# Two mixture-of-experts stages: a tile's biases copied on chip by a compute engine instead of fetched by two transfers

## The chip, the cores and the metric

The kernel runs on one core of one Trainium2 chip. The time is the device time of that core in microseconds (us), from repeated runs; 2293.36 us is the median before (3 runs, 2291.95 to 2298.7). A core has TensorE (PE in the profile: matrix products; PEld is its loading of weights), VectorE (DVE), ScalarE (ACT), GpSimd (POOL) and SyncE (SP), each with its own instruction queue in order, and 16 DMA engines that move what the queues issue. Engines wait for each other by counting semaphores.

## What is computed

A network of two blocks on an image batch of 8 x 128 channels x 32 x 32, 8192 tokens of 128 numbers. Each block has a convolutional attention part and a mixture of 8 experts, in which each token goes to its two best experts. Cut to the experts:

```
# block 0, for each token and its two experts e, weighted by its gate
h = x @ w1[e] + b1[e]
y = (silu(h @ wg[e] + bg[e]) * (h @ wv[e] + bv[e])) @ w2[e] + b2[e]
# block 1
y = gelu(x @ w1[e] + b1[e]) @ w2[e] + b2[e]
```

## The kernel before

The kernel is a chain of stages with a barrier behind each: project, attend and route (block 0), **experts** (layer 0), combine and convolve, attend and route (block 1), **experts** (layer 1), combine and store. `experts` (L1104) is one function that runs twice; `second` tells the layers apart. Below, the first experts stage is layer 0 and the second is layer 1.

The routing stage has written every token, once for each of its two experts, as a row of 130 numbers into `xd_dram`, sorted by expert into tiles of `SLOT` = 256 rows. There are `TILES` = 71 tiles. A table in on-chip memory gives for tile j the expert (row 0) and the place of its rows (row 1). The weights of all 8 experts lie on chip in `wres`, and so do their biases: `biases` (128 x 8 x 4) for the first product and `down_biases` (128 x 8 x 128) for the second. In layer 0 w1 is multiplied into wg and wv beforehand, so both layers have an up-projection from 128 to 4 x 128 and a down-projection back (from 2 x 128 in layer 0, from 4 x 128 in layer 1).

For each tile j, with ring place r = j mod 8 and parity p = j mod 2:

- **SP** (`load`, L1158): reads the expert e and the place u from the table into registers (L1159, L1160), then issues three transfers into ring place r: `rec[:, r, 0:4]` from `biases` (L1161), `rec[:, r, 4:]` from `down_biases` (L1162), `xr[:, r]` from `xd_dram` (L1163). All three count on the semaphore `loaded[r]`, 16 each, so `LOADS` = 48 (L1124). The first 8 loads go out at once; the load for tile j + 8 waits until `yo` of tile j is ready (L1170).
- **TensorE** transposes the tile (`turn`, L1181, waits for `loaded[r]`), multiplies by the four up blocks (`first`, L1191, waits for `xt_copied` and `w_copied`), and by the down blocks (`finish`, L1205, after a register load of e at L1206).
- **The up copy** (`turn` of ScalarE in layer 0, L1225; of VectorE in layer 1, L1250): the tile's up block of weights, 128 x 512, from `wres` to `up[:, p]`, after a register load of e (L1222, L1247). It raises `w_copied`. In layer 1 it stands in VectorE's queue ahead of the `xt` copy.
- **VectorE** copies the transposed tile to `xt` (L1256, in layer 1 with the norm's scale and shift, L1253).
- **ScalarE** applies silu (L1238) or gelu (L1233) with the bias from `rec`; in layer 0 VectorE adds the second bias from `rec` and multiplies (L1265).
- **VectorE** (`finish`, L1269) adds the down bias from `rec[:, r, 4:]` (L1271), takes the rows' places (L1274) and multiplies by the gates into `yo` (L1276); **GpSimd** sends `yo` to its places by two indirect transfers (L1286).

What sets the order is `over_tiles` (L1126): every engine but SP and GpSimd runs, tile by tile, `first` of tile j + 1, `turn` of tile j + 2, `finish` of tile j. So a tile is transposed and its up block copied two steps before it is finished:

```
            for r in range(RING):
                at(first, group, r + 1)
                at(turn, group, r + 2)
                at(finish, group, r)
```

Of the kernel before, what the change touches and what calls it, by code (L numbers as in the profile page):

```python
# [9 lines left out]
ACT = mybir.ActivationFunctionType  # L10
# [294 lines left out]
E = 8  # L305
# [47 lines left out]
def attend_and_route_first(nc, sb, sem, bank, w, X, XF, stacks0, parts_dram, v_dram, xd_dram, table, resident, to_fold, down):  # L353
# [66 lines left out]
    def wide(t):  # L420
        return t[:].unsqueeze(2).to_broadcast([C, G, E])
    LOADS = 16 * (len(Q_PARTS) + len(K_PARTS))

# [21 lines left out]
    with nc.Block() as block:  # L445
# [90 lines left out]
        def _(pe):  # L536
# [4 lines left out]
            def take_max(b, par, k, slot):  # L541

                h, c, half = k // 16, k // 2 % TC, k % 2
                if k % 64 == 0:
                    pe.wait_ge(qk_loaded[k // 64], b * LOADS)
                pe.matmul(bank[:, slot, :], qs[par][0:KB, h, c * C:(c + 1) * C],  # L546
# [557 lines left out]
def experts(nc, sb, sem, bank, w, layer, xd_dram, yd_dram, table, resident):  # L1104

    second = layer == 1
    wres, biases, down_biases = resident
    NH = 4 if second else 2
    W2 = 4 * C
    rec = sb("rec", [C, RING, BIASES], F32)  # L1110
    up = sb("up", [C, 2, 4 * C], F32)
# [7 lines left out]
    loaded = [sem(f"loaded{r}") for r in range(RING)]  # L1119
    turned, xt_copied, g_ready, v_ready, gated = sem("turned"), sem("xt_copied"), sem("g_ready"), sem("v_ready"), sem("gated")  # L1120
    w_copied = sem("w_copied")
    h_ready, y_ready, y_copied, yo_ready, held = sem("h_ready"), sem("y_ready"), sem("y_copied"), sem("yo_ready"), sem("held")
    sent = [sem("sent0"), sem("sent1")]
    LOADS = 16 * 3  # L1124

    def over_tiles(eng, turn, first, finish):  # L1126

        def at(step, group, r):
            group, r = group + r // RING, r % RING
            step(RING * group + r, r, r % 2, RING // 2 * group + r // 2, group)

        last = (TILES - 1) // RING
        at(turn, 0, 0)
        at(first, 0, 0)
        at(turn, 0, 1)
        with eng.Fori(0, last) as group:
# [4 lines that stand above are left out]
        left = TILES - last * RING  # L1144
        for r in range(left):
            if r + 1 < left:
                at(first, last, r + 1)
            if r + 2 < left:
                at(turn, last, r + 2)
            at(finish, last, r)  # L1150

    def nothing(*_):
        pass

    with nc.Block() as block:
        @block.sync
        def _(sp):
            def load(j, r):  # L1158
                e = sp.value_load(table[0:1, 0, bass.ds(j, 1)], min_val=0, max_val=E - 1)  # L1159
                u = sp.value_load(table[0:1, 1, bass.ds(j, 1)], min_val=0, max_val=UNITS_XD - 1)  # L1160
                sp.dma_start(rec[:, r, 0:4], biases[:, bass.ds(e, 1), :].rearrange("c o n -> c (o n)")).then_inc(loaded[r], 16)  # L1161
                sp.dma_start(rec[:, r, 4:], down_biases[:, bass.ds(e, 1), :].rearrange("c o n -> c (o n)")).then_inc(loaded[r], 16)  # L1162
                sp.dma_start(xr[:, r].rearrange("t q r -> t (q r)"),  # L1163
                             xd_dram[bass.ds(u * SLOT, SLOT), :].rearrange("(t q) r -> t (q r)", q=SQ)).then_inc(loaded[r], 16)

            for r in range(RING):
                load(r, r)

            def load_next(i, r):
                sp.wait_ge(yo_ready, RING * i + r + 1)  # L1170
                load(RING * (i + 1) + r, r)

            with sp.Fori(0, TILES // RING - 1) as i:
                for r in range(RING):
                    load_next(i, r)
            for r in range(TILES % RING):
                load_next(TILES // RING - 1, r)

        @block.tensor
        def _(pe):  # L1180
            def turn(j, r, p, h, i):  # L1181
                pe.wait_ge(loaded[r], (i + 1) * LOADS)
                pe.wait_ge(xt_copied, 2 * h)
                for q in range(SQ):
                    ins = pe.transpose(bank[:, p, q * C:(q + 1) * C], xr[:, r, q, 0:C], w["ident"])
                ins.then_inc(turned, 1)
# [30 lines left out]
        @block.scalar  # L1217
        def _(act):
            def turn(j, r, p, h, i):
                if second:  # L1220
                    return
                e = act.value_load(table[0:1, 0, bass.ds(j, 1)], min_val=0, max_val=E - 1)  # L1222
                if not (isinstance(j, int) and j < 2):
                    act.wait_ge(h_ready, (j - 1) * NH)
                act.activation(up[:, p], wres[:, bass.ds(e, 1), 0:W2].rearrange("c o n -> c (o n)"), ACT.Copy).then_inc(w_copied, 1)  # L1225

            def first(j, r, p, h, i):
                if not (isinstance(j, int) and j == 0):
                    act.wait_ge(y_ready, j - 1)
                for f in range(NH):  # L1230
                    act.wait_ge(g_ready, j * NH + f + 1)
                    if second:
                        act.activation(hidden[:, p, f, :], bank[:, 2 + f, 0:SLOT], ACT.Gelu,  # L1233
                                       bias=rec[:, r, f:f + 1]).then_inc(h_ready, 1)
                    else:
                        if f == 0:
                            act.wait_ge(h_ready, j * 2)
                        act.activation(gate[:, f, :], bank[:, 2 + 2 * f, 0:SLOT], ACT.Silu,  # L1238
                                       bias=rec[:, r, 2 * f:2 * f + 1]).then_inc(gated, 1)

            over_tiles(act, turn, first, nothing)

        @block.vector
        def _(dve):
            def turn(j, r, p, h, i):
                if second:
                    e = dve.value_load(table[0:1, 0, bass.ds(j, 1)], min_val=0, max_val=E - 1)  # L1247
                    if not (isinstance(j, int) and j < 2):
                        dve.wait_ge(h_ready, (j - 1) * NH)
                    dve.tensor_copy(up[:, p], wres[:, bass.ds(e, 1), 0:W2].rearrange("c o n -> c (o n)")).then_inc(w_copied, 1)  # L1250
                dve.wait_ge(turned, j + 1)
                if second:
                    dve.tensor_scalar(xt[:, p, :], bank[:, p, 0:SLOT], w["ln"][:, 0:1], w["ln"][:, 1:2],  # L1253
                                      ALU.mult, ALU.add).then_inc(xt_copied, 1)
                else:
                    dve.tensor_copy(xt[:, p, :], bank[:, p, 0:SLOT]).then_inc(xt_copied, 1)  # L1256

            def first(j, r, p, h, i):
                if not second:
                    if not (isinstance(j, int) and j == 0):  # L1260
                        dve.wait_ge(y_ready, j - 1)
                    for f in range(2):
                        dve.wait_ge(gated, j * 2 + f + 1)
                        dve.wait_ge(v_ready, j * 2 + f + 1)
                        dve.scalar_tensor_tensor(out=hidden[:, p, f, :], in0=bank[:, 3 + 2 * f, 0:SLOT],  # L1265
                                                 scalar=rec[:, r, 2 * f + 1:2 * f + 2], in1=gate[:, f, :],
                                                 op0=ALU.add, op1=ALU.mult).then_inc(h_ready, 1)

            def finish(j, r, p, h, i):  # L1269
                dve.wait_ge(y_ready, j + 1)  # L1270
                dve.tensor_tensor(y1[:, p], bank[:, 6 + p, 0:SLOT].rearrange("t (q c) -> t q c", q=SQ),  # L1271
                                  rec[:, r, 4:].unsqueeze(1).to_broadcast([C, SQ, C]), ALU.add).then_inc(y_copied, 1)
                dve.wait_ge(sent[p], h * (16 * SQ))
                dve.tensor_scalar(places[:, p], xr[:, r, :, C + 1], 0.0, None, ALU.add)  # L1274
                dve.wait_ge(y_copied, j + 1)
                dve.tensor_tensor(yo[:, p], y1[:, p], xr[:, r, :, C:C + 1].to_broadcast([C, SQ, C]), ALU.mult).then_inc(yo_ready, 1)  # L1276

            over_tiles(dve, turn, first, finish)
# [1012 lines left out]
def metaformer(nc, x_in, columns, weights, to_fold, rest0, rec1, toeplitz, out):  # L2291
# [31 lines left out]
    with ExitStack() as ctx:  # L2323
# [6 lines left out]
        with ExitStack() as own:  # L2330
            mine = allocator(own, nc.sbuf_tensor)
            XF, biases = mine("XF", [C, TOKENS], F32), mine("biases", [C, E, 4], F32)
            resident = (XF[:, 0:6 * T].rearrange("c (e k) -> c e k", e=E), biases[:],
                        XF[:, 6 * T:7 * T].rearrange("c (e k) -> c e k", e=E))
            with ExitStack() as first:
                stacks0 = [allocator(first, nc.sbuf_tensor)(name, [KM, HEADS, T], BF16)[:] for name in ("qs0", "ks0")]
                stage(normalize_and_project, X, XF, stacks0, parts_dram, v_dram)
                stage(attend_and_route_first, X, XF, stacks0, parts_dram, v_dram, xd_dram[0], table, resident, to_fold, rest0)
            stage(experts, 0, xd_dram[0], yd_dram[0], table, resident)
# [121 lines left out]
```

## Time and profile before

| | |
|---|---|
| runs, median (lowest to highest) | 2293.36 us (2291.95 to 2298.7) |
| the profiled execution: span | 2495.0 us, 41046 instructions |
| mean granted clock of TensorE | 0.887 of full speed |
| TensorE, VectorE, ScalarE, GpSimd busy | 80%, 57%, 44%, 30% of the span |
| the experts stages, layer 0 and layer 1 | about 1235 to 1520 us and 2131 to 2445 us of the span |

The profile shows one execution, recorded with all its instructions; for this one no other time than its span is shown, and it is longer than the runs that were timed without recording. Times in a timeline count from the span's start. A timeline row gives start, length, engine (SPq is the queue of SyncE), line of the kernel, operation, what is written and read, and in brackets the engine's idle time before it with what ended it. Register loads, waits and other instructions of the queues alone don't show in it. TensorE's products are pipelined and the ends of their rows are modelled; a run of them on one line is one row, with its count. A row of a group gives the line, the shapes, how many, the busy time in us, the mean length of one in ns, and the idle time ahead of them.

### The profile page before, as it was taken

How to read it: one execution, taken by the hardware profiler on the slowest of the kernel's cores; microseconds unless marked ns; L12 is line 12 of the kernel's file. 1: busy time of each engine (PE TensorE's matmuls, PEld its weight loads, DVE VectorE, ACT ScalarE, POOL GpSimd, SP SyncE). 2: the span in 40 equal slices, each digit the busy share in tenths (PEclk: the TensorE clock that was granted, in tenths of full speed). 3: DMA queues.
4: the chain of work that ended last, by engine and by line, in shares of the span. 5: the costliest groups of instructions: out<-in, count | busy, mean ns of one | idle time of the engine just before them, and what ended most of it. 6: DMA issues, size and time to landing. Idle time of an engine off the chain costs nothing. (4 is left out here: it accounts for less than half of the span.)

```text
span 2495.0 us, 41046 instructions
## 1 busy us (share of the span) xinstructions
PE 2001.3 (80%) x13306; PEld 1090.0 (44%) x13307; DVE 1432.7 (57%) x3154; ACT 1092.3 (44%) x1682; POOL 753.8 (30%) x883
## 2 busy tenths in 40 slices
PE   5759999898999899986588886986597871699894
PEld 2421223232232223223376664654365541588883
DVE  4779888686878687713155555742444453234444
ACT  4530666564656465763133443431143431334343
POOL 1240003332333334243244552000004445345442
PEclk9865999998999899987699998999889885799996
DMA  3844132323232322011333333222011321232325
GB/s 133 201 169 68 19 51 26 60 27 60 27 60 26 60 32 55 16 40 58 93 83 83 88 89 119 76 93 67 8 36 50 107 60 56 69 80 76 82 68 213
DMA packets 134782, 180.00 MB, mean 72 GB/s; under 512 B 44592, under 2 KB 87856, under 8 KB 132336
## 3 DMA queue, kind: packets, MB, share of 16 engines
q1 hardware_dynamic: 116208, 138.25, 23.3%
q0 software_dynamic: 18432, 39.88, 4.7%
q8 instruction: 87, 1.43, 0.2%
q14 instruction: 55, 0.45, 0.1%
HBM read 99.04 MB, written 69.01 MB: 67 GB/s over the span
## 5 line engine op out<-in xcount | busy, mean ns | idle before, releaser
L775 DVE TENSOR_REDUCE mx<-bank 128x1 f32<-128x512 f32 x1024 | 640.3, 696 | 140.3 <-PE bank L546 90.3
L722 ACT ACTIVATE P<-bank 128x1024 f32<-128x1024 f32 x512 | 498.0, 1021 | 412.9 <-PE bank L648 327.0
L546 PE MATMUL bank<-ks,qs 96*128 96x512 bf16 x1024 | 374.6, 415 | 62.7 <-DVE mx L775 44.3
L1286 POOL DMA_INDIRECT results<-yo,places x284 | 273.9, 964 | 359.6 <-DVE yo L1276 274.8
L648 PE MATMUL bank<-qs,ks 99*128 99x512 bf16 x1024 | 310.9, 387 | 14.3 <-ACT P L722 13.2
L1202 PE MATMUL bank<-xt,up 128*128 128x256 f32 x1136 | 286.6, 397 | 41.9 <-DVE xt L1253 20.8
L628 PE MATMUL bank<-P,vt 128*32 128x512 f32 x2048 | 277.5, 614 | 1.6 <-ACT P L722 1.6
L2285 POOL DMA_INDIRECT dispatched<-planes,places x128 | 123.1, 962 | 479.0 <-DVE stats L2129 356.3
L1202 PEld LDWEIGHTS bank<-xt,up 128*128 128x128 f32 x1136 | 211.6, 196 | 76.8 <-issue 36.0
L546 PEld LDWEIGHTS bank<-ks,qs 96*128 96x128 bf16 x1024 | 100.8, 99 | 305.7 <-DVE mx L775 204.0
L648 PEld LDWEIGHTS bank<-qs,ks 99*128 99x128 bf16 x1024 | 77.4, 98 | 299.1 <-ACT P L722 195.9
L1233 ACT ACTIVATE hidden<-bank,rec 128x256 f32<-128x256 f32 x284 | 121.0, 474 | 185.6 <-PE bank L1202 164.9
L995 POOL TENSOR_TENSOR a<-o,den 128x512 f32<-128x512 f32 x32 | 40.5, 1264 | 346.0 <-ACT den L710 322.8
L1211 PE MATMUL bank<-planes,hidden 128*128 x1136 | 141.8, 279 | 0.9 <-DVE y L1271 0.7
L1271 DVE TENSOR_TENSOR y<-bank,rec 128x256 f32<-128x256 f32 x142 | 60.1, 423 | 143.1 <-PE bank L1211 86.4
L1045 POOL DMA_INDIRECT dispatched<-outgoing,places x128 | 123.8, 967 | 44.9 <-issue 41.7
L1211 PEld LDWEIGHTS bank<-planes,hidden 128*128 128x128 f32 x1136 | 136.1, 196 | 1.4 <-issue 1.3
L1238 ACT ACTIVATE gate<-bank,rec 128x256 f32<-128x256 f32 x142 | 66.1, 473 | 149.5 <-PE bank L1202 102.2
L1713 PE MATMUL bank<-planes,bands 32*32 32x248 f32 (+2 forms) x3840 | 85.6, 394 | 43.0 <-issue 27.6
L1265 DVE SCALAR_TENSOR_TENSOR hidden<-bank,rec,gate 128x256 f32<-128x256 f32 x142 | 67.6, 483 | 61.9 <-ACT gate L1238 22.1
L1734 DVE STREAM_TRANSPOSE planes<-out 128x1024 f32<-128x1024 f32 x24 | 43.7, 1895 | 99.5 <-ACT out L1726 99.5
L1211 PE MATMUL bank<-XF,hidden 128*128 x568 | 80.5, 285 | 21.6 <-DVE hidden L1265 12.1
(298 smaller groups left out, 2582.3 us busy)
## 6 DMA issues: line engine op xcount, KB each, us to landing
xr<-dispatched SPq DMA_DIRECT2D x142, 130.0 KB
qk_parts<-parts SPq DMA_DIRECT2D x16, 768.0 KB, 5.1
qs<-qk_parts SPq DMA_DIRECT2D x84, 128.0 KB
ks<-qk_parts SPq DMA_DIRECT2D x84, 128.0 KB
v_turned<-vt SPq DMA_DIRECT2D x8, 1024.0 KB, 5.6
vt<-v_turned SPq DMA_DIRECT2D x8, 1024.0 KB
bands<-results SPq DMA_DIRECT2D x32, 256.0 KB, 3.8
y<-results SPq DMA_DIRECT2D x32, 256.0 KB
```

The costliest lines, as they stand in the source:

```text
L546: pe.matmul(bank[:, slot, :], qs[par][0:KB, h, c * C:(c + 1) * C], ks[par][0:KB, h, half * HALF:(half + 1) * HALF], start=True, stop=True) ...
L628: ins = pe.matmul(bank[32 * j:32 * j + 32, 4, :], vt[:, par, s, head * VH:(head + 1) * VH], P[:, (2 * e + j // 2) % SLOTS, j % 2 * HALF:(j ...
L648: ins = pe.matmul(bank[:, 2 * pair + u, :], ks[par][:, head, s * C:(s + 1) * C], qs[par][:, head, n * HALF:(n + 1) * HALF], start=True, st ...
L722: act.activation(P[:, x % SLOTS, :], bank[:, 2 * pair:2 * pair + 2, :] .rearrange("p a t -> p (a t)"), ACT.Exp).then_inc(probs_ready, 1)
L775: dve.tensor_reduce(mx[:, k // 2, k % 2:k % 2 + 1], bank[:, slot, :], AX.X, ALU.max).then_inc(unit_freed, 1)
L1045: pool.indirect_dma_start(xd_dram, bass.IndirectOffsetOnAxis(places[:, q, k:k + 1], 0), outgoing[:, q, k, :], None).then_inc(sent, 16)
L1202: ins = pe.matmul(bank[:, 2 + f, 0:SLOT], up[:, p, f * C:(f + 1) * C], xt[:, p, :], start=True, stop=True)
L1211: ins = pe.matmul(bank[:, 6 + p, q * C:(q + 1) * C], hidden[:, p, f, q * C:(q + 1) * C], weights(e, W2 + f * C), start=(f == 0), stop=(f = ...
L1233: act.activation(hidden[:, p, f, :], bank[:, 2 + f, 0:SLOT], ACT.Gelu, bias=rec[:, r, f:f + 1]).then_inc(h_ready, 1)
L1286: pool.indirect_dma_start(yd_dram, bass.IndirectOffsetOnAxis(places[:, p, q:q + 1], 0), yo[:, p, q, :], None).then_inc(sent[p], 16)
L1713: ins = pe.matmul(sums[:, :, y0:y1], bands[rows, m * TAPS + dy, :], plane[:, :, y0 + dy - PAD:y1 + dy - PAD], start=(dy == DY_ORDER[0]), s ...
L2285: pool.indirect_dma_start(xd_dram, bass.IndirectOffsetOnAxis(places[:, p, q, k:k + 1], 0), rows[p][:, q, k, :], None).then_inc(sent[p], 16)
```

## The change

The two transfers of `rec` and SP's register load of e are gone, and `LOADS` is 16. A new function `take_biases` copies the same two pieces, 128 x 4 and 128 x 128, from the resident biases to `rec[:, r]`. The engine that makes the up copy calls it right behind that copy, ScalarE in layer 0 (as an activation with the function Copy) and VectorE in layer 1 (as a tensor copy). `w_copied` is now raised by the second of the two copies instead of the up copy.

```
--- before.py
+++ after.py
@@ -1121,7 +1121,7 @@
     w_copied = sem("w_copied")
     h_ready, y_ready, y_copied, yo_ready, held = sem("h_ready"), sem("y_ready"), sem("y_copied"), sem("yo_ready"), sem("held")
     sent = [sem("sent0"), sem("sent1")]
-    LOADS = 16 * 3
+    LOADS = 16
 
     def over_tiles(eng, turn, first, finish):
 
@@ -1149,6 +1149,11 @@
                 at(turn, last, r + 2)
             at(finish, last, r)
 
+    def take_biases(copy, e, r):
+
+        copy(rec[:, r, 0:4], biases[:, bass.ds(e, 1), :].rearrange("c o n -> c (o n)"))
+        return copy(rec[:, r, 4:], down_biases[:, bass.ds(e, 1), :].rearrange("c o n -> c (o n)"))
+
     def nothing(*_):
         pass
 
@@ -1156,10 +1161,7 @@
         @block.sync
         def _(sp):
             def load(j, r):
-                e = sp.value_load(table[0:1, 0, bass.ds(j, 1)], min_val=0, max_val=E - 1)
                 u = sp.value_load(table[0:1, 1, bass.ds(j, 1)], min_val=0, max_val=UNITS_XD - 1)
-                sp.dma_start(rec[:, r, 0:4], biases[:, bass.ds(e, 1), :].rearrange("c o n -> c (o n)")).then_inc(loaded[r], 16)
-                sp.dma_start(rec[:, r, 4:], down_biases[:, bass.ds(e, 1), :].rearrange("c o n -> c (o n)")).then_inc(loaded[r], 16)
                 sp.dma_start(xr[:, r].rearrange("t q r -> t (q r)"),
                              xd_dram[bass.ds(u * SLOT, SLOT), :].rearrange("(t q) r -> t (q r)", q=SQ)).then_inc(loaded[r], 16)
 
@@ -1222,7 +1224,8 @@
                 e = act.value_load(table[0:1, 0, bass.ds(j, 1)], min_val=0, max_val=E - 1)
                 if not (isinstance(j, int) and j < 2):
                     act.wait_ge(h_ready, (j - 1) * NH)
-                act.activation(up[:, p], wres[:, bass.ds(e, 1), 0:W2].rearrange("c o n -> c (o n)"), ACT.Copy).then_inc(w_copied, 1)
+                act.activation(up[:, p], wres[:, bass.ds(e, 1), 0:W2].rearrange("c o n -> c (o n)"), ACT.Copy)
+                take_biases(lambda to, of: act.activation(to, of, ACT.Copy), e, r).then_inc(w_copied, 1)
 
             def first(j, r, p, h, i):
                 if not (isinstance(j, int) and j == 0):
@@ -1247,7 +1250,8 @@
                     e = dve.value_load(table[0:1, 0, bass.ds(j, 1)], min_val=0, max_val=E - 1)
                     if not (isinstance(j, int) and j < 2):
                         dve.wait_ge(h_ready, (j - 1) * NH)
-                    dve.tensor_copy(up[:, p], wres[:, bass.ds(e, 1), 0:W2].rearrange("c o n -> c (o n)")).then_inc(w_copied, 1)
+                    dve.tensor_copy(up[:, p], wres[:, bass.ds(e, 1), 0:W2].rearrange("c o n -> c (o n)"))
+                    take_biases(dve.tensor_copy, e, r).then_inc(w_copied, 1)
                 dve.wait_ge(turned, j + 1)
                 if second:
                     dve.tensor_scalar(xt[:, p, :], bank[:, p, 0:SLOT], w["ln"][:, 0:1], w["ln"][:, 1:2],
```

## Rows read from the trace of the kernel before

**Rows 1.** Windows by stage: busy us (and instructions) of each engine, PE clock, DMA share, GB/s.

```profile
1235.00:1520.00 285.00, 231.64 (x1278) 191.07 (x1278) 153.84 (x426) 112.03 (x214) 134.96 (x141) 0.96 0.31 83
...
2131.00:2445.00 314.00, 283.05 (x1846) 257.34 (x1846) 129.29 (x355) 122.28 (x285) 136.51 (x141) 0.95 0.28 75
```

**Rows 2.** Timeline of ScalarE, first stage: start, length, line, tiles [idle before, its releaser].

```profile
1251.55 0.47 ACT L1238 ACTIVATE gate<-bank,rec 128x256 f32<-128x256 f32 x1 [0.39 <-PE bank L1202]
1252.28 0.63 ACT L1225 ACTIVATE up<-XF 128x512 f32 x1 [0.26 <-issue]
```

**Rows 3.** Timeline of TensorE over the same tile.

```profile
1249.95 1.99 PE L1202 MATMUL bank<-xt,up 128*128 128x256 f32 x8
...
1253.15 1.56 PE L1202 MATMUL bank<-xt,up 128*128 128x256 f32 x6
```

**Rows 4.** Timeline of VectorE over the same tile.

```profile
1252.46 0.41 DVE L1256 COPY xt<-bank 128x256 f32<-128x256 f32 x1
```

**Rows 5.** Timeline of TensorE: first and last of the short distances.

```profile
1246.76 1.99 PE L1202 MATMUL bank<-xt,up 128*128 128x256 f32 x8 [0.70 <-DVE xt L1256]
...
1508.95 1.99 PE L1202 MATMUL bank<-xt,up 128*128 128x256 f32 x8
```

**Rows 6.** Timeline of SP's queue, start of the first stage.

```profile
1236.93 0.60 SPq L1161 DMA_DIRECT2D rec<-biases  x1
...
1238.42 0.43 SPq L1163 DMA_DIRECT2D xr<-dispatched  x1
1240.12 0.51 SPq L1161 DMA_DIRECT2D rec<-biases  x1
...
1243.18 0.50 SPq L1161 DMA_DIRECT2D rec<-biases  x1
```

**Rows 7.** Timeline of TensorE, start of the first stage.

```profile
1240.69 0.69 PE L1185 MATMUL bank<-weights,xr 128*128 128x128 f32 x2 [6.53 <-DMA xr<-dispatched]
```

**Rows 8.** Timeline of SP's queue, late in the first stage.

```profile
1417.94 0.50 SPq L1161 DMA_DIRECT2D rec<-biases  x1
...
1434.41 0.45 SPq L1163 DMA_DIRECT2D xr<-dispatched  x1
1436.61 0.50 SPq L1161 DMA_DIRECT2D rec<-biases  x1
```

**Rows 9.** Timeline of TensorE, late in the first stage.

```profile
1436.79 0.44 PE L1185 MATMUL bank<-weights,xr 128*128 128x128 f32 x2
```

**Rows 10.** Groups of ScalarE by shape: busy us, mean ns of one, idle before.

```profile
L1225 ACT ACTIVATE up<-XF 128x512 f32 x71 | 44.7, 630 | 19.7 <-issue 14.7 <-PEq L2315 3.5 <-DVE hidden L1265 1.4
...
L174 ACT ACTIVATE bqk<-weights 128x2 f32<-128x2 f32 x1 | 0.2, 203 | 7.5 <-PEq L2315 7.5
```

**Rows 11.** Groups of VectorE by shape.

```profile
L2113 DVE COPY ln_bias<-weights 128x128 f32<-128x128 f32 x1 | 0.2, 219 | 0.0
...
L2111 DVE COPY base<-weights 128x8 f32<-128x8 f32 x1 | 0.2, 159 | 0.0
```

**Rows 12.** Timeline of TensorE, second stage, two places.

```profile
2332.51 1.89 PE L1202 MATMUL bank<-xt,up 128*128 128x256 f32 x8
...
2336.25 1.89 PE L1202 MATMUL bank<-xt,up 128*128 128x256 f32 x8
...
2432.11 1.92 PE L1202 MATMUL bank<-xt,up 128*128 128x256 f32 x8
```

**Rows 13.** Timeline of VectorE, second stage, the same places.

```profile
2334.38 0.43 DVE L1250 COPY up<-planes 128x512 f32 x1 [0.42 <-ACT hidden L1233]
2334.72 0.54 DVE L1253 TENSOR_SCALAR xt<-bank,weights 128x256 f32<-128x256 f32 x1
...
2431.44 0.54 DVE L1253 TENSOR_SCALAR xt<-bank,weights 128x256 f32<-128x256 f32 x1
```

**Rows 14.** Timeline of ScalarE, second stage, a disturbed stretch.

```profile
2346.30 0.47 ACT L1233 ACTIVATE hidden<-bank,rec 128x256 f32<-128x256 f32 x1 [1.07 <-PE bank L1202]
2347.81 0.47 ACT L1233 ACTIVATE hidden<-bank,rec 128x256 f32<-128x256 f32 x1 [1.04 <-DMA bands<-toeplitz]
```

More of the change, by code:

```diff
@@ L1123, in experts @@
     sent = [sem("sent0"), sem("sent1")]
-    LOADS = 16 * 3
+    LOADS = 16
     def over_tiles(eng, turn, first, finish):
@@ L1150, in over_tiles, with take_biases @@
             at(finish, last, r)
+    def take_biases(copy, e, r):
+        copy(rec[:, r, 0:4], biases[:, bass.ds(e, 1), :].rearrange("c o n -> c (o n)"))
+        return copy(rec[:, r, 4:], down_biases[:, bass.ds(e, 1), :].rearrange("c o n -> c (o n)"))
     def nothing(*_):
@@ L1158, in load @@
             def load(j, r):
-                e = sp.value_load(table[0:1, 0, bass.ds(j, 1)], min_val=0, max_val=E - 1)
                 u = sp.value_load(table[0:1, 1, bass.ds(j, 1)], min_val=0, max_val=UNITS_XD - 1)
-                sp.dma_start(rec[:, r, 0:4], biases[:, bass.ds(e, 1), :].rearrange("c o n -> c (o n)")).then_inc(loaded[r], 16)
-                sp.dma_start(rec[:, r, 4:], down_biases[:, bass.ds(e, 1), :].rearrange("c o n -> c (o n)")).then_inc(loaded[r], 16)
                 sp.dma_start(xr[:, r].rearrange("t q r -> t (q r)"),
@@ L1224, in turn @@
                     act.wait_ge(h_ready, (j - 1) * NH)
-                act.activation(up[:, p], wres[:, bass.ds(e, 1), 0:W2].rearrange("c o n -> c (o n)"), ACT.Copy).then_inc(w_copied, 1)
+                act.activation(up[:, p], wres[:, bass.ds(e, 1), 0:W2].rearrange("c o n -> c (o n)"), ACT.Copy)
+                take_biases(lambda to, of: act.activation(to, of, ACT.Copy), e, r).then_inc(w_copied, 1)
             def first(j, r, p, h, i):
@@ L1249, in turn @@
                         dve.wait_ge(h_ready, (j - 1) * NH)
-                    dve.tensor_copy(up[:, p], wres[:, bass.ds(e, 1), 0:W2].rearrange("c o n -> c (o n)")).then_inc(w_copied, 1)
+                    dve.tensor_copy(up[:, p], wres[:, bass.ds(e, 1), 0:W2].rearrange("c o n -> c (o n)"))
+                    take_biases(dve.tensor_copy, e, r).then_inc(w_copied, 1)
                 dve.wait_ge(turned, j + 1)
```

## The prediction

> **What bounds the kernel now.** The windows by stage come first: the first experts stage lasts 285.00 us and the second 314.00 us of the span of 2495.0 us, at granted clocks of 0.96 and 0.95, so the upper of the two levels (2.4 GHz) nearly throughout [rows 1]. In the second, TensorE is busy for 283.05 of 314.00 us; in the first for 231.64 of 285.00 [rows 1]. Nothing outside these two stages is touched, so both are read tile by tile.
>
> In an undisturbed tile of the first stage, the chain runs over ScalarE. The up-projection starts at 1249.95 [rows 3]; the second gate starts at 1251.55 and ends at 1252.02, 2.07 us later; after 0.26 us for the register that holds the expert's number, the up copy runs from 1252.28 to 1252.91 [rows 2]; the next up-projection starts at 1253.15, 0.24 us behind it [rows 3]. That is 3.20 us per tile, all of it ScalarE's turn. VectorE's `xt` copy, the other operand, ends at 1252.87 [rows 4], only 0.04 us earlier.
>
> Later in the same stage something else shows. The queue of SP (SyncE) issues three transfers per tile. At the start it takes 3.06 us per tile with nothing to wait for (from 1240.12 to 1243.18) [rows 6]; later five tiles take from 1417.94 to 1436.61, 3.73 us each [rows 8]. There it has lost its lead: the 52nd `xr` is issued at 1434.41 [rows 8], and the 52nd pair of transposes starts at 1436.79, 2.4 us behind [rows 9], about the time that the first issue needs (1238.42 to 1240.69) [rows 6, 7]. So in this execution SP sets the pace over much of the stage.
>
> Is this pace that of the timed runs? The timed median is 2293.36 us; the profiled execution's span is 201.6 us longer. A stretch of the second stage shows where such time sits: ScalarE, with its operands long issued, starts activations of 0.47 us at 2346.30 and 2347.81, 1.51 us apart [rows 14]. I take these stalls, SP's extra 0.67 us per tile (3.73 less 3.06) among them, to belong to the recording, and the undisturbed tiles to the timed runs. The Trainium skill (Runtime: NRT & Kernel Launch, section The ~15µs preamble/postamble breakdown) states a gap of about 6.2 us that doesn't depend on the kernel; this trace disagrees with 201.6 us, but by that rule SP's pace would be real, which is the first rival below.
>
> **The change, part by part.** *Removed:* per tile, two issues and one register load on SP, and 66 KB of moving inside the on-chip memory. SP keeps one register load and one issue. From the start of the first issue to that of the third is 1.49 us (1236.93 to 1238.42); the two register loads lie in the 1.27 us between the third issue's end at 1238.85 and 1240.12, so one is 0.64 [rows 6]. The first `xr` of a stage is thus issued 2.1 us earlier, and the first transposes, which wait for nothing else (6.53 us, ended by that transfer [rows 7]), move with it. The second stage begins with the same pattern, once. What would be late next, the table load and the first up copy on the engine beside, ends before the first projection needs it. I take 1.95 us per stage: **-3.9 us**; bounds 0 and -4.2. Where SP isn't the pace, its remaining relief is worth nothing: it hides behind a tile of 3.20 us against SP's 3.06. The removed bytes are worth nothing either: the DMA engines are busy for 0.31 and 0.28 of the stages [rows 1].
>
> *Added in the first stage, on ScalarE:* two copies, 128x4 and 128x128, behind the up copy, with `w_copied` moved behind the second. The trace has no such copies of these sizes. The nearest are a 128x2 copy at 203 ns and the 128x512 one at 630 [rows 10]; a straight line between them gives about 205 and 310 ns, 0.51 us one after the other. But queued instructions overlap: on VectorE a copy of 0.43 us is followed 0.34 us later by the next [rows 13]. With some 0.1 us of overlap at each of two joints it is 0.28 to 0.31; I take **0.28 us**, since nothing separates the three copies but address arithmetic that the queue does while the 0.63 us copy runs. Behind them on ScalarE waits the next tile's gate, which waits for TensorE anyway; TensorE's own queue, in order, holds at `w_copied` the next up-projection, the transposes and the register load of the down-projection. So the chain goes from 3.20 to 3.48 us.
>
> How often does this count? At most for all 71 tiles: 71 x 0.28 = 19.9 us. At least where the profiled execution already has tiles closer than 3.47 us: 26 of the 70 distances between up-projections (the first begins at 1246.76, the last at 1508.95 [rows 5]), which fall short of it by 6.6 us together. I take the middle, **+13.3 us**: the timed runs should hold fewer disturbed tiles than the profile, but not none.
>
> *Added in the second stage, on VectorE:* the same two copies behind its up copy and ahead of `xt`. A 128x8 copy takes 159 ns and a 128x128 one 219 [rows 11]; less 0.09 at each joint that is 0.20 us, at worst 0.38. TensorE is the pace here: tiles start 3.74 us apart (2332.51 to 2336.25), while `xt`, begun at 2334.72, ends at 2335.26, 0.99 us ahead of its use [rows 12, 13]. That cover hides 0.20 us. Where VectorE runs late it is gone: another `xt` ends at 2431.98 and its projection starts at 2432.11 [rows 12, 13]. If every second tile were so, it would cost 35 x 0.20 = 7 us. I take **0**, as in the undisturbed tiles.
>
> Sum: -3.9 + 13.3 + 0 = +9.4 us. Against the profiled execution that is 2495.0 to 2504.4, and since the costs are in undisturbed tiles I add them whole to the median of the runs: 2293.36 + 9.4 = **2302.8 us**.
>
> **The rivals.** *SP's pace is real: faster.* If the timed runs also take 3.73 us per tile over some 50 tiles of the first stage [rows 8], the change replaces that by ScalarE's 3.48: 50 x 0.25 = 12.5 us less, and 3.9 at the starts: 2277 us. For it speaks the 2.4 us lead in rows 8 and 9; against it the 3.06 us that SP needs undisturbed [rows 6]. It decides from 3.48 us per tile on SP. Chance 0.22.
>
> *The copies are hidden: no change.* If only the 26 short distances count, the sum is +6.6 - 3.9 = +2.7: 2296 us. For it speaks that the stage's mean, 285.00/71 = 4.0 us [rows 1], has 0.5 us of room above 3.48; against it that a serial chain gives room only to those tiles that something else held up. Chance 0.28.
>
> *The copies don't overlap: clearly slower.* At 0.51 us on every tile it is 71 x 0.51 = 36.2, less 3.9: +32, 2326 us. The Trainium skill (VectorE: DVE Perf Modes, section The TRN2 errata — SBUF-src ops pay a fixed extra latency per instruction) speaks for it, and against this change: an instruction that reads SBUF pays a fixed cost exposed between instructions, so many small ones pay it each; its figures give an estimate of 0.48 us for the two copies on ScalarE, +30 us in all. The overlap in rows 13 disagrees. Chance 0.10.
>
> **How the numbers follow.** My own case, slower by 7 to 16 us, has 0.40. About 0.3%, 6.9 us, is what a measurement here can tell from no change. Faster by more: 0.22. Within: 0.28 of the hidden case. Slower: 0.40 + 0.10 = 0.50. The range reaches from the middle of the first rival, 2277 us, to short of the last, 2322 us (half of VectorE's worst on top of 19.9 and some lost overlap); about 0.1 lies out on each side. The likeliest case alone is 2298 to 2312 us.
>
> **What would show it.** Right: SP's two issues per tile gone, the first transposes of either stage 2 us earlier after SP's first register load; two new ScalarE groups of 71, near 0.2 and 0.3 us; the last copy of a tile ending some 0.9 us after its up copy began; and the shortest repeated distance of up-projections in the first stage 3.48 us where it is 3.20 now, with no transposes that wait for `xr`. In the second stage distances of 3.74 us as before. Wrong: if that shortest distance stays near 3.2 us, the copies cost nothing; if it is 3.7, they don't overlap; if the timed runs are faster although it is 3.48, SP was the pace in them.

## The result and the profile after

| | before | after |
|---|---|---|
| runs, median (lowest to highest) | 2292.6 us (2286.59 to 2299.22, 20 runs) | 2297.47 us (2293.47 to 2305.41, 20 runs) |
| ratio to before, 95% interval | | 1.0025 (1.0016 to 1.0033) |
| profiled execution: span | 2495.0 us | 2296.0 us (its own time 2297.84) |

The change makes the kernel 4.9 us slower by the medians. That is inside the 0.3% that the prediction called "within", on the side it forecast, and just below its likeliest case of 2298 to 2312 us.

The profile before was recorded on an execution some 200 us longer than the timed ones; this one agrees with the timed runs. Set side by side, the two spans would show a gain of 199 us that no timed run has. So "before" is read below from a second profile of the unchanged kernel (span 2283.4 us). First the changed kernel, in the windows of its two experts stages (columns as in [rows 1]):

```profile
1159.00:1420.00 261.00, 225.20 (x1297) 192.46 (x1296) 155.38 (x427) 134.75 (x357) 134.65 (x141) 0.99 0.25 73
...
1968.00:2250.00 282.00, 267.89 (x1846) 248.55 (x1846) 142.09 (x497) 126.61 (x285) 139.15 (x143) 0.98 0.23 67
```

One tile of the first stage, from the timeline of all engines (it answers [rows 2, 3]):

```profile
1284.27 1.99 PE L1204 MATMUL bank<-xt,up 128*128 128x256 f32 x8 [0.38 <-ACT rec L1228]
...
1285.86 0.47 ACT L1241 ACTIVATE gate<-bank,rec 128x256 f32<-128x256 f32 x1 [0.39 <-PE bank L1204]
...
1286.59 0.63 ACT L1227 ACTIVATE up<-XF 128x512 f32 x1 [0.25 <-issue]
1286.77 0.41 DVE L1260 COPY xt<-bank 128x256 f32<-128x256 f32 x1
1287.12 0.19 ACT L1228 ACTIVATE rec<-biases 128x4 f32 x1
1287.22 0.29 ACT L1228 ACTIVATE rec<-XF 128x128 f32 x1
1287.74 1.99 PE L1204 MATMUL bank<-xt,up 128*128 128x256 f32 x8 [0.38 <-ACT rec L1228]
```

The chain is the one of [rows 2, 3] with the two copies in it. The up copy begins at 1286.59, the last copy ends at 1287.51, 0.92 us later (forecast: some 0.9), and the next projection begins 0.23 us behind that. The distance is 3.47 us, and the bracket names the releaser: `rec`, at the line of the copies. Of the 70 distances of the stage 55 lie between 3.47 and 3.51 us. The groups of the new copies answer [rows 10, 11] (busy us, mean ns, idle before), first stage on ScalarE, second on VectorE:

```profile
L1228 ACT ACTIVATE rec<-XF 128x128 f32 x71 | 20.8, 293 | 0.0
L1228 ACT ACTIVATE rec<-biases 128x4 f32 x71 | 13.4, 189 | 0.0
```

```profile
L1155 DVE COPY rec<-planes 128x128 f32 x71 | 17.4, 245 | 0.1
L1154 DVE COPY rec<-planes 128x4 f32 x71 | 12.6, 177 | 0.0
```

The second stage (it answers [rows 12, 13]) keeps its pace. Its projections start 3.74 us apart, and `xt` ends at 2103.51, 0.65 us ahead of its use, though four instructions now stand where two were:

```profile
2100.42 1.89 PE L1204 MATMUL bank<-xt,up 128*128 128x256 f32 x8
2102.43 0.43 DVE L1253 COPY up<-planes 128x512 f32 x1 [0.92 <-ACT hidden L1236]
2102.77 0.16 DVE L1154 COPY rec<-planes 128x4 f32 x1
2102.84 0.44 DVE L1155 COPY rec<-planes 128x128 f32 x1
2102.97 0.54 DVE L1257 TENSOR_SCALAR xt<-bank,weights 128x256 f32<-128x256 f32 x1
2104.16 1.89 PE L1204 MATMUL bank<-xt,up 128*128 128x256 f32 x8
```

### The profile page after: what moved, and what is told of

Same layout as the page of the kernel before. It is cut to its first block and busy times, and to the rows that moved or that the text cites. A ratio compares the mean times of both kernels' runs of the same rounds, so it can differ in the third digit from the quotient of the medians.

```text
span 2296.0 us, 40508 instructions
## 1 busy us (share of the span) xinstructions
PE 1952.7 (85%) x13306; PEld 1076.5 (47%) x13307; DVE 1446.1 (63%) x3296; ACT 1119.5 (49%) x1824; POOL 756.3 (33%) x883
## 5 line engine op out<-in xcount | busy, mean ns | idle before, releaser
L1204 PE MATMUL bank<-xt,up 128*128 128x256 f32 x1136 | 278.7, 389 | 29.0 <-ACT rec L1228 26.1
L1204 PEld LDWEIGHTS bank<-xt,up 128*128 128x128 f32 x1136 | 207.0, 192 | 65.5 <-issue 38.0
L1717 PE MATMUL bank<-planes,bands 32*32 32x240 f32 (+2 forms) x3840 | 85.4, 392 | 42.2 <-issue 26.5
L1187 PE MATMUL bank<-weights,xr 128*128 128x128 f32 x284 | 54.9, 275 | 43.0 <-DMA xr<-dispatched 43.0
```

The source lines that it names most:

```text
L1204: ins = pe.matmul(bank[:, 2 + f, 0:SLOT], up[:, p, f * C:(f + 1) * C], xt[:, p, :], start=True, stop=True)
L1717: ins = pe.matmul(sums[:, :, y0:y1], bands[rows, m * TAPS + dy, :], plane[:, :, y0 + dy - PAD:y1 + dy - PAD], start=(dy == DY_ORDER[0]), s ...
```

## The experiments

**What did the kernel before do?** The unchanged kernel, profiled again; it took 2285.19 us in that run.

> The kernel before, unchanged, for a second profile. Theory A (the two queues take turns): in the changed kernel every tile of the first stage takes ScalarE's 3.48 us; the runs are 4.9 us apart in their medians, 3.9 of it given back at the starts, so the kernel before must average 3.48 less (4.9 + 3.9) / 70 = 3.35 us there, above ScalarE's 3.20 because SP's queue of three issues is the pace in the loop: distances all near 3.3, transposes that wait for xr, second stage 3.73. Theory B (disturbed tiles): distances of 3.20 in most tiles with single long ones between, which reach a mean near 3.35 by something that is not SP's queue. Theory C (SP as in the first profile): 3.73 in most tiles of the first stage, and the time is saved elsewhere.

First the start of the first stage in it, which answers [rows 6, 7], and then the same in the changed kernel:

```profile
1160.65 0.60 SPq L1161 DMA_DIRECT2D rec<-biases  x1
...
1162.14 0.43 SPq L1163 DMA_DIRECT2D xr<-dispatched  x1
1164.34 0.69 PE L1185 MATMUL bank<-weights,xr 128*128 128x128 f32 x2 [6.46 <-DMA xr<-dispatched]
1165.55 3.78 PE L1202 MATMUL bank<-xt,up 128*128 128x256 f32 x8 [0.52 <-DVE xt L1256]
```

```profile
1164.22 8.18 SPq L1165 DMA_DIRECT2D xr<-dispatched  x8
1166.35 0.69 PE L1187 MATMUL bank<-weights,xr 128*128 128x128 f32 x2 [4.40 <-DMA xr<-dispatched]
1167.55 3.45 PE L1204 MATMUL bank<-xt,up 128*128 128x256 f32 x8 [0.52 <-DVE xt L1260]
```

TensorE's wait falls from 6.46 to 4.40 us: 2.06 us gained (1.95 forecast). Then the queue of SP in the middle of the stage of the unchanged kernel, and TensorE beside it:

```profile
1288.93 0.43 SPq L1163 DMA_DIRECT2D xr<-dispatched  x1
...
1292.21 0.45 SPq L1163 DMA_DIRECT2D xr<-dispatched  x1
...
1295.99 0.43 SPq L1163 DMA_DIRECT2D xr<-dispatched  x1
...
1315.94 0.43 SPq L1163 DMA_DIRECT2D xr<-dispatched  x1
```

```profile
1289.88 1.91 PE L1202 MATMUL bank<-xt,up 128*128 128x256 f32 x8
1291.63 0.38 PE L1185 MATMUL bank<-weights,xr 128*128 128x128 f32 x2
1292.49 1.15 PE L1211 MATMUL bank<-XF,hidden 128*128 x8 [0.48 <-issue]
1293.48 1.89 PE L1202 MATMUL bank<-xt,up 128*128 128x256 f32 x8
...
1400.56 1.99 PE L1202 MATMUL bank<-xt,up 128*128 128x256 f32 x8
```

Eight loads, one turn of SP's loop, take from 1288.93 to 1315.94, 3.38 us each: 3.28 (1288.93 to 1292.21), and 3.78 across the loop's end (1292.21 to 1295.99). At the start, with nothing to wait for, a load takes 3.05 (3.06 in [rows 6]); in the loop each has a wait and its index arithmetic besides. The stage's up-projections run from 1165.55 to 1400.56, 235.01/70 = 3.36 us each. That is the 3.35 of theory A, and C falls: SP is the pace, at 3.38 us, not at the 3.73 of [rows 8]. The picture of B, most tiles at 3.20 us and single long ones, is not there either: in the loop short distances (3.1 to 3.3 us) and long ones (3.3 to 3.9 us) take turns.

Two signs of A failed with that: the distances are not all near 3.3 us, and the transposes show no wait for `xr`. The time stands elsewhere, as 0.48 us of "issue" ahead of the down products. The `xr` issued at 1288.93 has landed by the time TensorE itself is free for the transposes. But its queue was held by the wait for it until 1291.30, and the register load for the down products, next in that queue, begins at 1291.52; in the tile of the changed kernel shown above it begins at 1284.73, while the up-projection runs. (A queue's own instructions are in the trace, though the timeline leaves them out.) It is so in 48 tiles on end, the 17th to the 64th up-projection: the register load begins 2.27 to 2.63 us behind the issue of the `xr` that the queue waits for. In the changed kernel it begins some 16.5 us behind that issue, and 0.37 to 0.47 us behind the start of the up-projection. In the groups of TensorE in the first stage this idle time is there before, and gone after, where ScalarE's copies take its place:

```profile
L1211 PE MATMUL bank<-XF,hidden 128*128 x552 | 78.1, 284 | 13.8 <-issue 7.8 <-DVE hidden L1265 4.2
```

```profile
L1204 PE MATMUL bank<-xt,up 128*128 128x256 f32 x568 | 142.6, 395 | 27.6 <-ACT rec L1228 26.1 <-issue 1.1 <-DVE xt L1260 0.5
L1213 PE MATMUL bank<-XF,hidden 128*128 x552 | 72.9, 275 | 0.0
```

**The two halves of the change apart.** Three kernels made of the changed one. *Copies off the chain:*

```
-                act.activation(up[:, p], wres[:, bass.ds(e, 1), 0:W2].rearrange("c o n -> c (o n)"), ACT.Copy)
-                take_biases(lambda to, of: act.activation(to, of, ACT.Copy), e, r).then_inc(w_copied, 1)
+                act.activation(up[:, p], wres[:, bass.ds(e, 1), 0:W2].rearrange("c o n -> c (o n)"), ACT.Copy).then_inc(w_copied, 1)
+                take_biases(lambda to, of: act.activation(to, of, ACT.Copy), e, r).then_inc(b_copied, 1)
...
             def first(j, r, p, h, i):
                 if not (isinstance(j, int) and j == 0):
                     act.wait_ge(y_ready, j - 1)
+                if not second:
+                    act.wait_ge(b_copied, j + 1)
```

> The changed kernel with the two copies of the first stage off the chain: the up copy raises w_copied itself, the copies raise a semaphore of their own that ScalarE's gate waits for. Theory A: 3.20 us per tile where the changed kernel has 3.48, so 71 x 0.28 = 19.9 us less than its 2297.5: 2277.6 us, ratio to before 0.9935. Theory B: only the undisturbed tiles gain, at most half: about 2288, ratio 0.998. If the copies' time on ScalarE itself counts (the next gate is late), no gain: 2297, 1.002.

*Transfers kept,* into a tile that nothing reads, with `LOADS` at 48 again, so that TensorE waits for all three:

```
+    spare = sb("spare", [C, RING, BIASES], F32)
...
+                e = sp.value_load(table[0:1, 0, bass.ds(j, 1)], min_val=0, max_val=E - 1)
+                sp.dma_start(spare[:, r, 0:4], biases[:, bass.ds(e, 1), :].rearrange("c o n -> c (o n)")).then_inc(loaded[r], 16)
+                sp.dma_start(spare[:, r, 4:], down_biases[:, bass.ds(e, 1), :].rearrange("c o n -> c (o n)")).then_inc(loaded[r], 16)
```

> The changed kernel with SP's load of e and its two transfers kept, into a tile that nothing reads, so the copies are paid and nothing is removed. Theory A: 3.48 us per tile as in the changed kernel (SP's 3.3 is hidden behind it), and 1.95 us more at each start: 2297.5 + 3.9 = 2301.4, ratio to before 1.004. Theory C (SP takes 3.73 us per tile): 71 x 0.25 = 17.8 us more on top: 2319, ratio 1.011.

*Both edits:*

> Both edits: the transfers kept and the copies off the chain. Theory A: SP's pace as in the kernel before, about 3.35 us per tile, and its starts: 2292.6 us, ratio 1.000 (0.999 to 1.001). Theory B: the same time as the kernel with the copies off the chain plus 3.9 us.

Each cell has the median, the ratio to the runs of the kernel before that were taken beside it, with its interval, and the mean distance of up-projections in the first stage of the profile (last start less first, over 70):

| | copies ahead of `w_copied` | copies off the chain |
|---|---|---|
| transfers gone | the change: 2297.47 us, 1.0025 (1.0016 to 1.0033), 3.50 us | 2277.57 us, 0.9943 (0.9924 to 0.9962), 3.22 us |
| transfers kept | 2299.86 us, 1.0043 (1.0029 to 1.0056), 3.50 us | 2294.1 us, 1.0021 (1.0001 to 1.0040), 3.36 us |

Theory A holds in all four cells. With the copies on the chain SP's load is hidden: keeping it costs only the starts. SP's queue then runs ahead of TensorE at a pace of its own, which is 3.38 us again (eight loads in 27.00 us), and its lead over the transposes grows from 5.40 us at the 17th tile to 11.28 at the 65th:

```profile
1270.15 0.44 SPq L1169 DMA_DIRECT2D xr<-dispatched  x1
...
1297.15 0.43 SPq L1169 DMA_DIRECT2D xr<-dispatched  x1
```

With the copies off the chain, SP's load is the pace again, at 3.36 us as in the kernel before. Only with neither does the tile come to 3.22. The last kernel (transfers kept, copies off the chain) was expected at 1.000; its interval just leaves that out. One of its twelve runs, at 2316.99 us, is 21 us above all others and lifts the ratio; its first stage is that of the kernel before, and where the rest lies stays open. The tile with the copies off the chain and the transfers gone (the window ends within its last row):

```profile
1272.42 1.99 PE L1204 MATMUL bank<-xt,up 128*128 128x256 f32 x8
...
1274.74 0.63 ACT L1227 ACTIVATE up<-XF 128x512 f32 x1 [0.25 <-issue]
1274.92 0.41 DVE L1262 COPY xt<-bank 128x256 f32<-128x256 f32 x1
1275.27 0.19 ACT L1228 ACTIVATE rec<-biases 128x4 f32 x1
1275.37 0.29 ACT L1228 ACTIVATE rec<-XF 128x128 f32 x1
...
1275.60 1.77 PE L1204 MATMUL bank<-xt,up 128*128 128x256 f32 x7
```

The projection at 1275.60 starts 0.23 us behind the up copy's end (1275.37) and ahead of the last copy's end: 3.18 us, against 3.47 with the copies waited for. The copies' price is thus 0.29 us a tile.

**The number of issues, or the bytes?** Copies off the chain, as above, but only the 128x4 piece copied; the 128x128 piece (64 KB) stays SP's transfer, with its register load.

```
+                e = sp.value_load(table[0:1, 0, bass.ds(j, 1)], min_val=0, max_val=E - 1)
+                sp.dma_start(rec[:, r, 4:], down_biases[:, bass.ds(e, 1), :].rearrange("c o n -> c (o n)")).then_inc(loaded[r], 16)
...
     def take_biases(copy, e, r):
-        copy(rec[:, r, 0:4], biases[:, bass.ds(e, 1), :].rearrange("c o n -> c (o n)"))
-        return copy(rec[:, r, 4:], down_biases[:, bass.ds(e, 1), :].rearrange("c o n -> c (o n)"))
+        return copy(rec[:, r, 0:4], biases[:, bass.ds(e, 1), :].rearrange("c o n -> c (o n)"))
```

> Copies off the chain as in the earlier run, but only the 128x4 piece is copied; the large piece (64 KB) stays a transfer of SP, with SP's load of e. If the pace of the kernel before is the number of issues on SP's queue (3.38 us per tile in the loop of the second profile, one issue 0.65), SP needs 2.73 us per tile, less than ScalarE's 3.20, and the whole gain of the loop stays: 2277.6 us and 1.35 us more at each start, 2280.3, ratio to before 0.995. If it is the bytes moved or the landing of the large transfer, the tile stays near 3.36 us: about 2291, ratio 1.000.

Measured: 2281.79 us, 0.9947 (0.9926 to 0.9968), 3.23 us per tile; the wait of the first transposes is 5.62 us. Nearly all of the moved bytes are back, and the gain stays: SP's count of issues was the pace. SP's queue at the start of the stage, two loads:

```profile
1163.77 0.44 SPq L1166 DMA_DIRECT2D xr<-dispatched  x1
...
1166.17 0.43 SPq L1166 DMA_DIRECT2D xr<-dispatched  x1
```

One issue less makes 2.40 us of the 3.05. The Trainium skill (Perfetto Trace Analysis, section What "DMA-bound" means) knows this bound as that of the sequencer, with a track of solid DMA slices as its sign and large descriptors as the cure. The sign is not there: in the unchanged kernel three issues of 0.50, 0.49 and 0.43 us fill 1.42 of 3.28 us, and register loads, the wait and arithmetic the rest. Nor was size what counted here: the issues of the 2 KB and of the 64 KB piece took 0.50 and 0.49 us, and leaving out the smaller one removed the bound. Larger descriptors were not tried.

**More copies on the chain.** In the changed kernel, the pair is made twice in the first stage and four times in the second.

```
+        for n in range(3 if second else 1):
+            copy(extra[:, n, r, 0:4], biases[:, bass.ds(e, 1), :].rearrange("c o n -> c (o n)"))
+            copy(extra[:, n, r, 4:], down_biases[:, bass.ds(e, 1), :].rearrange("c o n -> c (o n)"))
         copy(rec[:, r, 0:4], biases[:, bass.ds(e, 1), :].rearrange("c o n -> c (o n)"))
```

> The changed kernel with more copies on the chain: in the first stage the two copies are made twice, in the second four times (the further ones into a tile that nothing reads). If each pair adds 0.28 us to ScalarE's chain: 3.76 us per tile in the first stage, 20 us more. If VectorE's cover in the second stage holds (some 0.9 us against 3 x 0.2), distances there stay 3.73 us: 2297.5 + 20 = 2317, ratio to before 1.011. If the cover is smaller than 0.6 us, the second stage grows too, up to 71 x 0.6 = 43 us: 2360, ratio 1.030.

Measured: 2320.48 us, 1.0127 (1.0073 to 1.0181). First stage, ScalarE:

```profile
1283.49 0.19 ACT L1232 ACTIVATE extra<-biases 128x4 f32 x1
1283.58 0.29 ACT L1232 ACTIVATE extra<-XF 128x128 f32 x1
1283.78 0.19 ACT L1232 ACTIVATE rec<-biases 128x4 f32 x1
1283.88 0.29 ACT L1232 ACTIVATE rec<-XF 128x128 f32 x1
1284.40 1.99 PE L1208 MATMUL bank<-xt,up 128*128 128x256 f32 x8 [0.67 <-ACT rec L1232]
```

From one pair to the next (1283.49 to 1283.78) it is 0.29 us, though the durations add up to 0.48; the distance of tiles is mostly 3.77 or 3.78, and the stage grows by some 22 us (20 expected). The Trainium skill (VectorE: DVE Perf Modes, section The TRN2 errata — SBUF-src ops pay a fixed extra latency per instruction) has a fixed cost exposed between such instructions; these rows disagree. The lengths of a pair add up to the 0.48 us that the prediction's estimate had, but each copy begins 0.09 to 0.20 us after the one ahead of it, before that one has ended. In the second stage 53 of 70 distances stay at 3.73 or 3.74 us with three more pairs; only two tiles in eight grow (3.92 and 3.83 us, where VectorE's loop turns over). So its cover held for 0.2 us and nearly for 0.8.

**A register load, as a probe of the pace.** ScalarE reads the register for the next tile's up copy ahead of its gates, where it waits anyway; put into the kernel before, the changed one, and the one with the copies off the chain. In the edit, `expert(j)` is that register load.

```
             def first(j, r, p, h, i):
+                if not second and not (isinstance(j, int) and j == TILES - 1):
+                    following["e"] = expert(j + 1)
...
             def turn(j, r, p, h, i):
-                e = act.value_load(table[0:1, 0, bass.ds(j, 1)], min_val=0, max_val=E - 1)
+                e = following.pop("e", None)
+                if e is None:
+                    e = expert(j)
```

In the kernel before:

> The kernel before with the early register alone: 0.26 us less on ScalarE's chain, SP's three issues as they were. If SP's queue is the pace of the kernel before (3.38 us per tile in its loop), nothing is gained but in the first tiles, before SP's lead is used up: 2291, ratio to before 1.000 (0.998 to 1.001). If ScalarE's chain is the pace there, tiles go from 3.20 towards 3.05 us, as with the copies off the chain: 10 us less, ratio 0.996.

In the changed kernel:

> The changed kernel with the early register alone, the copies still ahead of w_copied. ScalarE's chain is its pace, so 3.48 - 0.26 = 3.22 us per tile: 71 x 0.26 = 18.5 us less than 2297.5: 2279, ratio to before 0.994. The same edit that is worth nothing in the kernel before is then worth 18 us here. If something else paced the changed kernel: 2297, ratio 1.0025.

In the one with the copies off the chain:

> Copies off the chain, and ScalarE reads the register for the next tile's up copy ahead of its gates, where it waits anyway. The 0.26 us between second gate and up copy go from ScalarE's chain; VectorE's xt is 0.04 us behind it and takes over: 3.16 us per tile, 70 x 0.04 = 2.8 us less than with the copies off the chain alone: 2274.8, ratio to before 0.993. If TensorE's own work is the pace at 3.19, no difference: 2277.6.

| the early register in | median | ratio to before | distance, first stage |
|---|---|---|---|
| the kernel before | 2293.24 us | 1.0009 (0.9999 to 1.0019) | 3.36 us, as without it |
| the changed kernel | 2271.19 us | 0.9916 (0.9902 to 0.9931) | 3.13 us (3.50) |
| copies off the chain | 2267.19 us | 0.9883 (0.9844 to 0.9922) | 3.06 us (3.22) |

The same edit is worth nothing in the kernel before and some 25 us in the changed one (1.0025 less 0.9916). That ScalarE's chain is no bound in the one, and the bound in the other, is thereby shown. The gain was 0.37 us a tile, not 0.26: the up copy now even overlaps the gate ahead of it. In the last kernel the next bound appears (again the window ends within the last row):

```profile
1273.04 1.99 PE L1204 MATMUL bank<-xt,up 128*128 128x256 f32 x8
...
1275.01 0.62 ACT L1234 ACTIVATE up<-XF 128x512 f32 x1
1275.08 1.06 PE L1213 MATMUL bank<-XF,hidden 128*128 x8
...
1275.54 0.41 DVE L1271 COPY xt<-bank 128x256 f32<-128x256 f32 x1
...
1276.09 1.12 PE L1204 MATMUL bank<-xt,up 128*128 128x256 f32 x4
```

No idle time is left in TensorE's rows; tiles are 3.05 us apart. The expected 3.16 missed: it took the handoff from VectorE (0.14 us, from 1275.95 to 1276.09) to be as long as that from ScalarE (0.23), which is 0.09 of the 0.11 us. Whether `xt` or TensorE's own work sets this last pace is not separated. This version beats both kernels, by 1.2% of the kernel before.

## Why the prediction came out as it did

- **The sign and the place: right.** The first stage lost time on ScalarE's chain, both stages won at the start, the second kept its pace.
- **The price of the copies: right.** 0.28 us was taken, 0.29 measured; 3.48 us per tile was forecast and is there in nearly every tile.
- **The starts: right.** -3.9 us; measured -2.06 in the first stage. In the second the wait of the first transposes was 40.35 to 41.02 us in four profiles with the three transfers and 38.13 to 38.56 in five without them: about -2.2. That is -4.3 in all, just past the bound of -4.2.
- **The second stage: right.** 0 was taken. The 0.99 us of cover became 0.65 in the tile shown, and 0.2 us never came through.
- **The number of tiles that pay: wrong, and with it the size.** "I take the middle, +13.3 us" between 6.6 and 19.9. All tiles paid the 0.29 us, against a chain of 3.20 us. But the kernel before did not run at 3.20: it ran at 3.36, held by SP. The term is 244.69 - 235.01 = +9.7 us. That the middle came near it was luck: its reason, disturbed tiles, was not there.
- **The step that failed** is "Where SP isn't the pace, its remaining relief is worth nothing: it hides behind a tile of 3.20 us against SP's 3.06". The 3.06 was read at the start, where SP's loads wait for nothing. In its loop the same load takes 3.28, and 3.38 with the loop's end. So the relief was worth 0.14 us a tile (3.36 to 3.22 with the copies off the chain), and the copies on ScalarE's chain cost twice that.
- **What was put down to the recording: half wrong.** Of SP's extra 0.67 us a tile, 0.32 (3.38 less 3.06) is there in an execution as long as the timed ones. That the recording made the first execution some 200 us longer isn't shown either: in the two later profiles the span is 1.8 us shorter than the execution's own time. What held the first one up stays open.
- **The first rival was half right.** SP was the pace in the timed runs too, as 2.4 us of lead in [rows 8, 9] had said. Its 3.73 us was not; at 3.38 it stays below the 3.48 from which, as the prediction had it, that rival decides. The second rival's time, 2296 us, lies nearest to the measured one, but its reason fell: not 26 tiles paid for the copies, all did. The third fell with the overlap.

The terms, -4.3 + 9.7 - 0.5 (the second stage's loop, 264.20 to 263.72 us, all of it between its first two projections), come to +4.9 us, the measured difference of the medians. That they meet it so closely is luck in part: the two profiled executions are 12.6 us apart, and 8.0 of that lies outside both stages, where nothing was changed.

## What to carry to other kernels

Read a queue's pace inside its loop, not in the stretch ahead of it: a wait, its arithmetic and the loop's end made a 3.05 us load one of 3.38. When two paces lie within a few tenths of a us, relieving one engine by loading another trades one for the other, so put the new work behind the signal that the chain waits for, with a semaphore of its own: here that alone turned +0.25% into -0.57%. And try a probe that shortens only one chain: whether it pays tells which chain is the bound.

## What the hardware did that was not expected

- A late transfer can show as idle time ahead of an instruction that doesn't use it: 0.48 us of "issue" ahead of the down products, because the queue could not reach its next register load.
- In the second stage of the kernel with more copies, VectorE's copies of 0.16 and 0.22 us follow each other 0.07 and 0.13 us apart, so that three further pairs cost some 0.6 us and nearly vanish behind the cover.
- A register load on ScalarE's chain costs more than the idle time ahead of the next instruction (0.25 us): taken away it gave 0.37 us a tile of the changed kernel (3.50 to 3.13), as the up copy then overlaps the gate ahead of it.
